# Setup loads of a four-layer transformer kernel issued in another order and from other engines

## What is computed

```
x = L0(x, ctx, cond)   # adaptive layer norm by silu(cond) @ Wss + bss, cross attention (16 heads)
x = L1(x, cond, ctx)   # evidence attention over ctx, router of 3 experts on [nx, evidence, cond]
x = L2(x, cond, ctx)   # modulation silu(cond) @ W_mod, self attention, cross attention, MLP
x = L3(x, cond, ctx)   # modulation silu(cond) @ w_ada, window attention, top-16 cross attention, gated MLP
```

```
silu(cond) @ [Wss_q | Wss_kv | W_mod | w_ada] + biases      # the modulation columns
cond @ e_w1[:, 2D:3D], gate_w1[2D:3D], router_W[2D:3D]      # the "anchor" part of L1
(ctx @ Wv) @ e_w1[:, D:2D], gate_w1[D:2D], router_W[D:2D]   # the "evidence" part of L1
ctx @ W_kvc, ctx @ w_kv, ctx @ Wk, LN(ctx) modulated @ Wkv  # keys and values
```

## Time and profile before

| | us |
|---|---|
| median of 3 runs | 1656.64 |
| the profiled execution | 1657.31 |
| its span in the profile | 1655.5 |
| PE busy | 1524.2 (92%) |
| DVE busy | 1049.4 (63%) |
| ACT busy | 770.6 (47%) |
| POOL busy | 378.9 (23%) |

### The profile page before, as it was taken

One profiled execution on the slowest core, in us unless ns is written; L12 is line 12 of the kernel. 1 busy time (PEld: TensorE's weight loads), 2 busy tenths in 40 slices (PEclk: granted clock), 3 DMA queues, 4 the chain that ended last, 5 costly groups with the idle time before them and its releaser, 6 DMA issues.

```text
span 1655.5 us, 26452 instructions
## 1 busy us (share of the span) xinstructions
PE 1524.2 (92%) x10523; PEld 927.3 (56%) x10523; DVE 1049.4 (63%) x2946; ACT 770.6 (47%) x1228; POOL 378.9 (23%) x419
## 2 busy tenths in 40 slices
PE   5899998999998999978998999899999899897898
PEld 3447674444444856656774657543444476665676
DVE  3573344999727446799457434499991744679953
ACT  1334421688853533335543543148886354333444
POOL 3510006343006000114124000344400701001320
PEclk9899999999999999999999999999999999999999
DMA  9400006221020000000040000542202000000000
GB/s 340 142 1 1 0 33 154 36 38 31 2 77 1 1 0 2 2 1 2 20 147 1 0 1 0 150 61 40 40 2 77 1 1 1 3 2 1 1 1 26
DMA packets 37551, 59.62 MB, mean 36 GB/s; under 512 B 7360, under 2 KB 26979, under 8 KB 36531
## 3 DMA queue, kind: packets, MB, share of 16 engines
q1 hardware_dynamic: 25239, 34.71, 6.3%
q0 software_dynamic: 9408, 15.85, 6.1%
q10 hardware_dynamic: 2780, 7.36, 1.2%
HBM read 42.03 MB, written 2.10 MB: 27 GB/s over the span
## 4 chain that ended last, share of the span: by engine, by line
PE 65%; DVE 22%; issue 6%; ACT 3%; SPq 1%; POOL 1%; DMA 1%; DVEq 0%; POOLq 0%; ACTq 0%
PE ps L993 9%; PE ps L1005 9%; PE ps L464 6%; PE ps L1302 4%; DVE taken L2359 3%; PE ps L978 3%; PE ps L870 3%; PE ps L1092 3%; PE ps L1100 3%; DVE taken L2371 3%; DVE rs L2045 2%; PE ps L848 2%; DVE m L2354 2%; DVE mxw L2037 2%; PE ps L592 2%
## 5 line engine op out<-in xcount | busy, mean ns | idle before, releaser
L2230 DVE TENSOR_REDUCE mm<-ps 128x1 f32<-128x1024 f32 x256 | 310.3, 1223 | 32.8 <-PE ps L978 25.6
L1623 ACT ACTIVATE pt<-ps 128x512 f32<-128x512 f32 x512 | 276.8, 599 | 59.1 <-PE ps L993 41.4
L2477 POOL TENSOR_TENSOR rstd<-ve,minus_half 128x4 f32<-128x4 f32 x32 | 35.7, 1114 | 747.1 <-DVE ve L1909 747.1
L993 PE MATMUL ps<-qx,kx 64*128 64x512 f32 x512 | 188.4, 445 | 1.0 <-ACT pt L1623 1.0
L978 PE MATMUL ps<-kx,qx 48*128 48x512 f32 x512 | 186.7, 444 | 0.2
L1005 PE MATMUL ps<-pt,v 128*32 128x256 f32 x2048 | 158.7, 390 | 0.0
L993 PEld LDWEIGHTS ps<-qx,kx 64*128 64x128 f32 x512 | 78.9, 184 | 95.9 <-ACT pt L1623 85.9
L2120 DVE TENSOR_TENSOR rlo<-ring,rhi 128x512 fp32r<-128x512 f32 x48 | 33.2, 692 | 119.7 <-ACT ring L1573 119.7
L592 PE MATMUL ps<-filler 128*128 128x512 f32 x300 | 94.5, 433 | 0.0
L1005 PEld LDWEIGHTS ps<-pt,v 128*32 128x32 f32 x2048 | 42.9, 108 | 85.7 <-ACT pt L1623 61.6
L978 PEld LDWEIGHTS ps<-kx,qx 48*128 48x128 f32 x512 | 75.3, 184 | 22.1 <-issue 18.1
(11 more groups left out here) (373 smaller groups left out, 3359.7 us busy)
## 6 DMA issues: line engine op xcount, KB each, us to landing
wm<-in_L_xcond_W_mlp_dram SPq DMA_DIRECT2D x4, 1024.0 KB, 8.9
qx<-q_hi POOLq DMA_DIRECT2D x64, 64.0 KB, 2.6
kx<-k_hi POOLq DMA_DIRECT2D x64, 64.0 KB, 2.8
w3a<-in_L_xcond_w_m_dram SPq DMA_DIRECT2D x2, 2048.0 KB, 8.0
w<-in_L_xcond_e_w_dram SPq DMA_DIRECT2D x6, 512.0 KB, 7.0
w<-in_L_xcond_e_w_dram SPq DMA_DIRECT2D x2, 1536.0 KB, 13.2
s_ada<-in_L_xcond_w_ada_dram ACTq DMA_DIRECT2D x1, 2304.0 KB, 22.6
qx<-q_lo POOLq DMA_DIRECT2D x32, 64.0 KB, 2.6
```

Of the source, the lines that this page charges most:

```text
L993: pe.matmul(ps[:, bank, :], kx[r, p % 4, kc * P:(kc + 1) * P], qx[r, p % 4, half * 512:(half + 1) * 512], start=True, stop=True).then_inc( ...
L1623: act.activation(pt[:, u % 8, half * 512:(half + 1) * 512], ps[:, bank, :], ACT.Exp, scale=QK_SCALE).then_inc(st_read, 1)
L2230: return dve.tensor_reduce(mm[:, p % 2, e, t:t + 1], place(), X, ALU.max).then_inc(ring_read, 1)
```

## The change

Bias rows: SP loads vectors 0 to 15 instead of 0 to 11, GpSimd 16 to 23 instead of 12 to 23 (four ahead of its power and four behind), and ScalarE's five move from behind s_q1 to the front of its queue. s_mod and s_ada move from ScalarE to SP, ahead of x. The five anchor loads move from SP to the end of ScalarE's loads, behind s_kv0. The counts in PE's waits follow. Nothing of the computation is changed.

```diff
 # SP
-            load_rows(sp, 0, 12, rows_ld[0])
+            load_rows(sp, 0, 16, rows_ld[0])
+            for tile, name in ((s_mod, "L2_xcond_W_mod"), (s_ada, "L3_xcond_w_ada")):
+                sp.dma_start(tile[:, :, :], rows(g[name])).then_inc(s_mod_ld, 16)
...
             load_x(0, 0)
             load_x(0, 1)
-            for e in range(E):
-                sp.dma_start(s_an[:, e, :, :], rows(g["L1_xcond_e_w1"][e, 2 * D:3 * D, :])).then_inc(s_an_ld, 16)
-            sp.dma_start(s_gan[:, :, :], rows(g["L1_xcond_gate_w1"][2 * D:3 * D, :])).then_inc(s_an_ld, 16)
-            sp.dma_start(s_ran[:, :, :], rows(g["L1_xcond_router_W"][2 * D:3 * D, :])).then_inc(s_an_ld, 16)
 # PE
-            pe.wait_ge(rows_ld[0], 12 * 16)
-            pe.wait_ge(rows_ld[1], 12 * 16)
+            pe.wait_ge(rows_ld[0], 16 * 16)
+            pe.wait_ge(rows_ld[1], 8 * 16)
 # ScalarE
+            load_rows(act, 24, len(vectors), rows_ld[2])
             for tile, name in ((s_kvc, "L2_xcond_W_kvc"), (s_kv3, "L3_xcond_w_kv"), (s_k1, "L1_xcond_Wk"), (s_v1, "L1_xcond_Wv")):
                 act.dma_start(tile[:, :, :], rows(g[name])).then_inc(s_kv_ld, 16)
             act.dma_start(s_q1[:, :, :], rows(g["L1_xcond_Wq"])).then_inc(s_q_ld, 16)
-            load_rows(act, 24, len(vectors), rows_ld[2])
-            for tile, name in ((s_ss_q, "L0_xcond_Wss_q"), (s_ss_kv, "L0_xcond_Wss_kv"), (s_mod, "L2_xcond_W_mod"),
-                               (s_ada, "L3_xcond_w_ada")):
+            for tile, name in ((s_ss_q, "L0_xcond_Wss_q"), (s_ss_kv, "L0_xcond_Wss_kv")):
                 act.dma_start(tile[:, :, :], rows(g[name])).then_inc(s_mod_ld, 16)
             act.dma_start(s_kv0[:, :, :], rows(g["L0_xcond_Wkv"])).then_inc(s_kv0_ld, 16)
+            for e in range(E):
+                act.dma_start(s_an[:, e, :, :], rows(g["L1_xcond_e_w1"][e, 2 * D:3 * D, :])).then_inc(s_an_ld, 16)
+            act.dma_start(s_gan[:, :, :], rows(g["L1_xcond_gate_w1"][2 * D:3 * D, :])).then_inc(s_an_ld, 16)
+            act.dma_start(s_ran[:, :, :], rows(g["L1_xcond_router_W"][2 * D:3 * D, :])).then_inc(s_an_ld, 16)
 # GpSimd
-            load_rows(pool, 12, 18, rows_ld[1])
+            load_rows(pool, 16, 20, rows_ld[1])
...
-            load_rows(pool, 18, 24, rows_ld[1])
+            load_rows(pool, 20, 24, rows_ld[1])
```

## The result

The changed kernel took 1663.55 us in the median of 21 runs, the kernel before 1657.1 in 21: ratio 1.0036, 95% interval 1.0024 to 1.0048, so 4 to 8 us slower.

What follows compares the result with a forecast made beforehand. The kernel was taken to wait first for loads, later for its own work. ScalarE's block until 30.0 us moves L531 from 37.32 to 49.5, +12.1 on 1656.6: 1668.7 us; own range 1665 to 1673, widened to 1656 to 1676.

Steps and rivals of the forecast that it cites:

- rival 1: Setup, ScalarE's queue: ScalarE isn't blocked and s_ran sets the end; +5.5 us, 1662.1; chance 0.14.
- (a): Front of ScalarE's queue: five bias DMAs delay all weights there by 2.0 us; rows land sooner, no gain counted.
- (b): SP's issues: four more row DMAs, so s_mod goes out at about 7.0 us, s_ada at 7.5, x behind.
- (c): s_mod and s_ada on SP's queue share one for one with ScalarE's; s_ada and s_q1 carried at 21.7 us.
- s_q before 12 us: Sign in the profile after: if s_q lands before 12 us, the sharing between queues is not one for one.
- (d): Anchor DMAs on ScalarE: the full queue blocks it until 30.0 us instead of 8.40; set_act 1 at 32.8.
- What stands behind the block: ScalarE's table load and copies of s_ctxT, queued behind the blocked issue, for which PE waits: 2.76 us.
- (e): PE from L489: 10.57 us to L524 at 43.4, then 6.1 to L531 at 49.5 instead of 37.32, +12.1 us.
- The 1.7 us given back by the higher level: Between L524 and L531: PE arrives without a pause, so the first 3.9 us or so run faster, saving 1.7 us.
- (f): From L531 to L600: no DMA wait ended last before, so 20 us of work stays 20 us.
- 2, faster by a better order: Setup loads: better order brings L531 before 37.3 us; gains 4.3 us at most, taken as 2, 1654.6; chance 0.12.
- 3, nothing changes: Setup loads: the queues' order doesn't matter, as all share the DMA engines; 1656.6; chance 0.08.

Runs made afterwards that it cites:

- e4: Kernel before with only the bias rows moved (ScalarE's five first, SP 16 instead of 12, GpSimd 8 instead of 12); ratio 1.0001.
- e9: Changed kernel with s_mod and s_ada issued ahead of SP's sixteen bias rows; main body starts at 67.77 us against 64.25, one run.
- e3: Kernel before with only the five anchor loads moved from SP to behind s_kv0 on ScalarE; ratio 1.0052.
- e5: Changed kernel with anchor loads read as rows of twice the length, same bytes; main body starts at 55.72 us against 64.25, one run.
- e7: Kernel before with s_mod and s_ada on SP ahead of everything but the bias rows, and x behind s_rev; ratio 0.9983.
- e2: Kernel before with only s_mod and s_ada moved to SP ahead of x; ratio 1.0001, main body starts at 59.61 us.
- e11: e2 with four useless matmuls ahead of the wait for the anchors; main body starts at 55.69 us against 59.61, one run.
- e1: Changed kernel with the five anchor loads issued behind ScalarE's first compute; ratio 1.0020 against the kernel before.
- e10: e2 with nine useless matmuls ahead of the wait for the anchors; main body starts at 62.28 us against 59.61, one run.

## Why the prediction was right

It said slower by 12.1 us, 1668.7, in 1656 to 1676. Measured were 6.4 by the medians (1663.55), with a setup that is 6.9 us longer. The mechanism is right. The sum is nearly twice too large: 4.5 us of the excess are in the length of the block and 0.8 in the modulation rows, and L598 came at 64.25, not near 69. The measured median lies below the forecast's own 1665 to 1673 and in rival 1's 1659 to 1664; it is inside 1656 to 1676 because that range had been widened to take in rivals 1 and 3. Step by step:

- (a) Five bias DMAs first: 2.0 us were expected until s_kvc's issue, it moved from 0.74 to 2.65, 1.9. The part alone costs nothing (e4).
- (b) s_mod at 7.0 and s_ada at 7.5: issued at 7.13 and 7.58. Its cover, that DVE wants x late, holds.
- (c) **The step that failed.** It put the first large row at 8.2 us, with 743 + 30 packets carried by ScalarE's queue, so that s_q1 had to share to its end and would land near 22. By 8.2 us it had carried 899, and then q1 carried almost nothing until 10.6 us (382 packets at 8.2, 413 at 10.6). Its first packet of 6 KB came at 10.94, 3.8 us after the issue of s_mod rather than 1.2. From 8.2 to 10.6 q10, with little opposite, carried 710 more, 296 a microsecond, and stood at 1609. s_q1 landed at 11.3. By the prediction's own sign, s_q before 12 us, the sharing would not be one for one; it was, as soon as the large rows ran (373 and 368 packets), and it was their start that was wrong. e9, where the large rows come early, shows what the step had assumed for this kernel: a late landing (27 us) and a long block (31.5).
- (d) The block. The mechanism is as told, with the issue of s_ran ending at 25.45, not 30.0. From 1609 at 10.6, 609 packets more brought it there, 41 a microsecond. The prediction has this rate too, 537 in 13.5 us, but only until 21.7 us, when s_ada should be through, and 118 from there on, a rate beside rows of 1 KB. s_ada landed at 29.4, and the large rows stood opposite to the end of the block. Too few carried at the start and too fast a rate behind it: the two errors partly cancel. The limit was 1140 at that issue against my 1065 to 1120; e3 shows that it can be 1384. e5 shows that it counts rows.
- What stands behind the block: 2.76 us from its end to the copies' end expected, 28.24 - 25.48 = 2.76 measured.
- (e) 10.57 us for the keys: 38.98 - 28.38 = 10.60. The modulation rows to their transposes: 6.1 expected, 44.25 - 38.98 = 5.27 measured. The 1.7 us given back by the higher level were right: the rows themselves took 7.03 us before and 5.27 after. The other 0.8 was a wait for s_ran, which the prediction had read as work of PE and which fell away:

```profile
37.32 1.59 PE L531 MATMUL ps<-ident,s_mrow 128*128 128x128 f32 x12 [0.79 <-DMA s_ran<-in_L_xcond_router_W_dram]
```

- (f) 20.0 us from there to the main body: 64.25 - 44.25 = 20.0. Nothing of it was absorbed later; 7.1 us at 90 us, 7.2 at 280.

The sum with the block as measured: 25.48 + 2.76 + 10.6 + 5.3 + 20.0 = 64.1.

The rivals. 1, ScalarE isn't blocked, is refuted by the 9.37 us of s_gan's issue, although its time, 1662.1, lay nearer to what was measured than mine: a time alone would have pointed to the wrong cause. 2, faster by a better order, was decided where it said: the transposes were not ahead of 37.3. e7 shows that there was something in it, 3.6 us of setup, once x goes last and the anchors stay off ScalarE. 3, nothing changes, with the rule of the Trainium skill behind it (page "DMA: Bandwidth & Descriptors", section "Issuing engines are not separate DMA queues"), is refuted by e3, where five transfers change nothing but their queue and their place in it and the time goes up by 0.52%. The rule's reason, that all share the same 16 DMA engines, holds in the traces; its conclusion, that only the sequencer's time is at stake and is small, does not hold here, since that time was 15 us and lay on the chain.

Open: what sets the room of a queue exactly, why the large rows of the changed kernel started so late, and why the dip in the evidence matmuls falls in some executions. A mark is one execution.

## What to carry to other kernels

A DMA issued from a computing engine is free only as long as its queue has room. Count the contiguous rows that an engine issues ahead of its first compute, here room was for some 1000 to 1400 (896 to 1581 at the extremes), and put loads that aren't wanted soon behind that compute, or on an engine that computes nothing, or read them in longer rows. Order loads by when they are wanted, not by size, and look at what stands opposite in the other queues: here they took turns by packets, so that q1 with its 6 and 9 KB rows moved 2.85 MB while q10 moved 0.71.

## What the hardware showed that I had not expected

- A queue's room is counted in rows and not sharply: in six traces 30 issues of 2 us and more ended with 1007 to 1385 rows outstanding, and reading the same 5.26 MB in 2956 packets instead of 3596 moved the end of the block from 25.45 us to 11.38.
- A load's first large packet can come late: 3.8 us after the issue of s_mod in the changed kernel (7.13, then 10.94), while ScalarE's queue carried some 300 packets a microsecond, 2.6 in e2 and 1.2 in e9, where the queues had only begun (1.65, then 2.84). What holds it back no run shows.
- An idle stretch of 4.25 us (e2) let TensorE fall from 2.4 to 1.2 GHz; filling 3.70 us of it with useless matmuls (e11) kept it at the higher level, worth 2.8 us. Behind idle stretches of 1.2 to 1.9 us (e11, e1) it stayed there; behind one of 2.54 us (e10) it began at the higher level and was at the lower from 28.5 to 31.9 us.
- The same kernel's runs spread over 15 us (1656.97 to 1671.89), and the mean granted clock roughly goes with it, 0.981 to 0.974. Effects of a few microseconds have to be read at a mark in the trace, and even there one dip of the clock is worth 1.7 us.
